# Attention with decay bias and a gated feed-forward block: projections in two runs of four per head, weighing in one run, maxima placed one head earlier

## What is computed

```python
qkv = layernorm(x) @ w_attn + b_attn            # 32 heads of width 16
scores = einsum('bqhd,bkhd->bhqk', q, k) / 16
scores = where(rel <= 0, scores + slopes * rel, -inf)   # rel = key position - query position
out = softmax(scores) @ v
x = x + out @ w_proj + b_proj
```

## Time and profile before

| | us |
|---|---|
| median of 3 runs | 922.75 |
| lowest, highest | 920.37, 922.88 |
| profiled execution | 921.12 |
| its span, first to last instruction | 919.4 |
| TensorE busy (matmul) | 860.3 |
| VectorE busy | 477.3 |
| ScalarE busy | 364.1 |
| GpSimd busy | 183.5 |

### The profile page before, as it was taken

The page is one execution under the profiler, slowest core; times in us unless marked ns, Lnnn a source line. Parts: engine busy times, 40 slices in busy tenths (PEclk is TensorE's granted clock), DMA queues, the critical chain, the costliest instruction groups (busy, mean ns, idle before and its releaser), DMA issues. The chain is left out here.

```text
span 919.4 us, 13759 instructions
## 1 busy us (share of the span) xinstructions
PE 860.3 (94%) x5088; PEld 580.1 (63%) x5088; DVE 477.3 (52%) x931; ACT 364.1 (40%) x693; POOL 183.5 (20%) x337
## 2 busy tenths in 40 slices
PE   1999799999999999999998579999999999999998
PEld 1755355556555565555543268887888788878886
DVE  6586577766777667776773154443222322232223
ACT  4345455565556655565555233322111211111111
POOL 4223233342433324333342300000000000000000
PEclk9999899999999999999999879999999999999999
DMA  8764445655565455735461364203000310021001
GB/s 267 207 208 140 122 146 170 185 155 161 177 207 164 137 171 186 227 112 170 143 207 49 113 227 155 89 0 137 2 1 1 96 41 0 0 77 60 0 0 46
DMA packets 70562, 109.33 MB, mean 119 GB/s; under 512 B 13395, under 2 KB 38662, under 8 KB 70505
## 3 DMA queue, kind: packets, MB, share of 16 engines
q1 hardware_dynamic: 68457, 108.32, 37.5%
q10 hardware_dynamic: 2048, 0.27, 0.2%
HBM read 65.97 MB, written 42.32 MB: 118 GB/s over the span
## 5 line engine op out<-in xcount | busy, mean ns | idle before, releaser
L839 DVE TENSOR_REDUCE bm<-bank 128x3 f32<-128x384 f32 (+1 forms) x384 | 223.0, 596 | 118.8 <-PE bank L1045 114.7
L700 ACT ACTIVATE pt<-bank 128x512 f32<-128x512 f32 (+1 forms) x384 | 196.8, 528 | 168.4 <-PE bank L1067 162.9
L1067 PE MATMUL bank<-q_st,k_st 116*128 116x512 bf16 (+3 forms) x512 | 136.7, 309 | 18.0 <-DMA q_st<-mt 10.5
L1336 DVE TENSOR_TENSOR gu<-bank,silu 128x512 f32<-128x512 f32 x44 | 30.5, 692 | 220.2 <-issue 132.7
L1147 PE MATMUL bank<-fT_hi,wgu_hi 128*128 128x512 f32 x352 | 138.8, 394 | 5.5 <-DVE wgu_lo L1308 3.5
L1043 PE MATMUL bank<-k_st,q_st 97*128 97x512 bf16 (+3 forms) x512 | 141.6, 302 | 0.8 <-DMA q_st<-slopes_dram 0.6
L1147 PE MATMUL bank<-fT_lo,wgu_hi 128*128 128x512 f32 x352 | 138.4, 393 | 0.0
L1147 PE MATMUL bank<-fT_hi,wgu_lo 128*128 128x512 f32 x352 | 137.7, 391 | 0.0
L1067 PEld LDWEIGHTS bank<-q_st,k_st 116*128 116x128 bf16 x512 | 41.7, 98 | 131.0 <-ACT pt L700 72.1
L1045 PE MATMUL bank<-mask_qk,identb 128*128 128x128 bf16 x512 | 106.4, 220 | 0.0
L610 POOL TENSOR_SCALAR_AFFINE_SELECT pt<-pt 128x256 f32<-128x256 f32 x128 | 52.7, 412 | 213.1 <-ACT pt L700 213.1
(11 more groups left out here) (95 smaller groups left out, 1217.0 us busy)
## 6 DMA issues: line engine op xcount, KB each, us to landing
stack_dram<-part SPq DMA_DIRECT2D x32, 384.0 KB, 2.6
q_st<-stack_dram SPq DMA_DIRECT2D x32, 384.0 KB
k_st<-stack_dram SPq DMA_DIRECT2D x32, 384.0 KB
stack_dram<-part SPq DMA_DIRECT2D x32, 256.0 KB, 3.1
pv_dram<-weighed SPq DMA_DIRECT2D x32, 256.0 KB, 4.8
weighed<-pv_dram SPq DMA_DIRECT2D x17, 256.0 KB
xt<-x SPq DMA_DIRECT2D x16, 256.0 KB, 4.3
stack_dram<-part SPq DMA_DIRECT2D x32, 128.0 KB, 3.9
```

The lines of the kernel that those rows point to most:

```text
L700: act.activation(pt[:, h % PT_RING, COL0[k]:COL0[k] + WIDE[k]], bank[3 + (3 * h + k) % 2][:, 0:WIDE[k]], ACT.Exp, scale=1.0 / HD).then_inc ...
L839: dve.tensor_reduce(bm[:, h % 4, BM_AT[k]:BM_AT[k] + BM_N[k]], bank[k][:, 0:BM_N[k] * P].rearrange("p (n q) -> p n q", q=P), AX.X, ALU.max ...
L1067: last = pe.matmul(bank[3 + u % 2][:, at:at + n], k_st[0:K_EXP, s, h % 4, t * P:(t + 1) * P], q_st[0:K_EXP, s, h % 4, t * P:S], start=True ...
L1336: dve.tensor_tensor(gu[:, f % 2, :], bank[5 + 2 * (f % 2)][:, :], silu[:, f % 2, :], ALU.mult).then_inc(gu_done, 1)
```

## The change

- TensorE, each head: the projections stand behind the shifted scores of k = 0 and k = 1, four each, ahead of the scores of the same k. Before they stood behind the scores, three, three and two.
- The pair of shifted scores of k = 1 is issued the other way round, 128 columns (t = 3) and then 384 (t = 1); each keeps its place in the bank.
- The weighing of the chunk before runs as a whole behind the scores of head 0, k = 1. Before, t = 0 stood there and the rest behind k = 2.
- The next chunk's maxima are transposed behind the scores of head 1, k = 0 (before: after head 1), copied behind the maximum of head 1, k = 1 (before: of head 2, k = 0), and placed after the exponentials of head 1 (before: of head 2).
- ScalarE copies the weighed values (`copy_pv`) after the third exponential of head 0; before, after the first of head 1.

```diff
@@ ScalarE
-                    if i == 1 and c > 0:
-                        copy_pv(c - 1)
...
                     exponential(h, 2)
+                    if i == 0 and c > 0:
+                        copy_pv(c - 1)
+                    if i == 1 and c + 1 < CHUNKS:
+                        place_maxima(c + 1)
...
                     if i == 2:
-                        if c + 1 < CHUNKS:
-                            place_maxima(c + 1)
@@ VectorE
                     scored(0)
-                    if i == 2 and c + 1 < CHUNKS:
-                        copy_maxima(c + 1)
                     if i == 3:
                         for tile in made(c)[:1]:
                             read_tile(*tile)
                     scored(1)
+                    if i == 1 and c + 1 < CHUNKS:
+                        copy_maxima(c + 1)
@@ shifted_scores
-                at = 0
-                for t in T_TILES[k]:
+                for t in T_TILES[k][::-1]:
                     n = S - t * P
+                    at = S - P if t == 3 else 0
...
-                    at += n
@@ TensorE
                         shifted_scores(h, k)
+                        if i > 0 and k < 2:
+                            between(c, 8 * (i - 1) + 4 * k, 8 * (i - 1) + 4 * k + 4)
                         scores(h + AHEAD, k)
-                        if i > 0:
-                            between(c, 8 * (i - 1) + 3 * k, 8 * (i - 1) + min(3 * k + 3, 8))
-                        if i == 0 and c > 0:
-                            if k == 1:
-                                weigh_values(c - 1, (0,))
-                            if k == 2:
-                                weigh_values(c - 1, (1, 3, 2))
+                        if (i, k) == (0, 1) and c > 0:
+                            weigh_values(c - 1, (0, 1, 3, 2))
+                        if (i, k) == (1, 0) and c + 1 < CHUNKS:
+                            transpose_maxima(c + 1)
...
-                    if i == 1 and c + 1 < CHUNKS:
-                        transpose_maxima(c + 1)
```

## The result

The changed kernel takes 915.32 us as the median of 20 runs, the kernel before 921.47 us beside it; the ratio is 0.9929, with a 95% interval of 0.9915 to 0.9942. That is 6.5 us less by the ratio and 6.2 by the medians. The prediction was 911 (899 to 921) and a gain of 10.7 by its sum: the sign and the range hold, the gain was forecast too large. The profiled execution took 915.61 us with a span of 913.9, 5.5 under that of before.

A forecast was written before the change was run, and what follows sets the result against it. TensorE, busy for 94% of the span, was taken as the bound. Terms -13.2 - 5.0 + 11.7 - 3.8 - 0.6 - 2.0 + 1.5 + 0.7 = -10.7 us gave 910.4 or 912.1, predicted as 911 us, range 899 to 921.

The forecast's parts named there:

- the projections: Two runs of four behind wide shifted scores save entry costs, 0.17 us per head in 26 x 3 heads: -13.2 us.
- the weighing: One run instead of two in first heads saves 0.2 us in each of 25 chunks (1, 4 to 27): -5.0 us.
- the held-up exponential: Later scores delay exponential (h,1): 1.03 us stalls ending nine chunks, 0.6 after 9, 17, 25; with chunk 1, +11.7 us.
- the stacks: K's later second part delays the stack loads for chunks 8, 16 and 24, 0.5 us taken each: +1.5 us.
- the cover of what stands behind it on VectorE: In chunk 2 of a batch, P's second tile enters earlier and the tokens' low part comes later: 0.25 us three times, +0.7.
- Chunk 1: At its end TensorE waits for VectorE's normalised tokens; the delayed remainder adds +0.6 us, with no clock priced.
- The chunks without projections: In chunks 2, 3 and 28 to 31 ScalarE bounds, so one weighing run gains 0 (-1 to +2).
- The maxima: Earlier placing removes waits in the loop's body: -3.8 us, with -0.6 at chunk 4 and -2.0 before chunk 30.
- 2 us more until the next chunk's first score: Issue on ScalarE's queue moves from 10.4 us into its chunk to about 7.8 of 13.7, leaving 2 us more for landing.
- Rival B: In the second head ScalarE's issue waits for VectorE's copy, TensorE pays in every chunk: 925 to 926 us, slower; chance 0.13.

The follow-up runs named there:

- the experiment that cuts it: The changed kernel with VectorE making a Q tile's remainder ahead of the block maximum of k = 0 in head 3: 907.31 us, ratio 0.9859.

## Why the prediction was right, and where it was off

The sign and the range held, and so did the mechanism of the three largest terms (the projections, the weighing, the held-up exponential); of the gain of 10.7 us 6.2 to 6.5 arrived. Between the two traces 5.2 us are missing: 3.6 in chunks 0 to 3, 2.3 in chunks 4 to 27 and 0.5 before the loop, less 1.1 that the end of the loop gave beyond its forecast. Two misses helped, and that is luck: the 1.5 us for the stacks were not due in this trace, and chunk 4's first head lost 1.1 us of lower clock.

**The projections: right, a little small.** Forecast 0.17 us a head, measured 0.17 in second heads (3.48 for 3.65) and 0.20 in third ones (3.20 for 3.40); the bounds from the mask and from the rows of chunk 31 carried over to tiles with scores in them, and the reversed order is worth what the prediction said it would be.

**The weighing: right in size, incomplete around it.** Forecast 0.2, measured 0.23 to 0.24 in most first heads (3.73). The step that failed is the cover of what stands behind it on VectorE: the prediction put 0.25 us on chunk 2 of a batch, three times. In the second and third heads of chunks 10, 18 and 26 the changed kernel has 4.16 and 3.68 us, where the sum gives 3.92 and 3.23: 0.7 together in each of these chunks. The low part of the tokens is late both times, once for the second transposes (0.24) and once for P's second tile (0.45). Chunk 10's third head, where P's second tile starts just after VectorE has written the low part (L815):

```profile
210.32 0.67 DVE L815 TENSOR_TENSOR fT_lo<-bank,fT_hi 128x512 fp32r<-128x512 f32 x1
...
211.09 0.47 PE L1003 MATMUL bank<-wproj_hi,aT_hi 128*128 128x512 f32 x1 [0.22 <-issue]
```

The sum had nothing for the chunks behind them, 12 and 20, either. Their first heads take 4.45 and 4.38 us (4.10 and 4.19 before) and their third ones 3.60 (3.40): in chunk 12 VectorE reads a P tile (L829) only after a wait of 1.51 us for GpSimd, the maximum comes behind it, and TensorE waits for that. Some 2 us together; no run here takes that apart.

```profile
231.23 0.69 DVE L829 TENSOR_TENSOR xr<-bank,xr 128x512 f32<-128x512 f32 x1 [1.51 <-POOL xr L619]
...
232.44 0.34 PE L1043 MATMUL bank<-k_st,q_st 97*128 97x384 bf16 x1 [0.54 <-DVE bm L839]
```

**The held-up exponential: right.** Forecast 4.25 for the last heads of nine chunks and of chunks 9, 17 and 25; measured 4.27 in eight of them, 4.36 in chunks 5, 13 and 21, and 5.00 in chunk 23, because VectorE there first waits 1.20 us for the load of the values that it divides. The chain was taken from the earlier trace rows alone, and the experiment that cuts it gives the time back.

**Chunk 1: right in kind, too small.** Forecast +0.6 for the tokens, measured +0.84 at the end of chunk 1. But the sum priced no clock for a longer wait, on the ground that 1.21 us had left it up. That was the argument for the new stalls of 1.0 us, and there it held: the clock stays up through all of them. The wait before chunk 2 was another one, 1.54 us in the kernel before and longer after, and I didn't look at it. It cost 1.7 us, the largest single miss.

**The chunks without projections: in the bounds.** Forecast 0 (-1 to +2). Placing in head 1 holds ScalarE by its 1.15 us where ScalarE is the bound: chunk 2's third head grows by 1.2 us and the last one falls by 0.8 (with the placement late again the third is back at 1.84). Its second head grows by 0.9 us too, but that belongs to the weighing: it takes 3.06 with the weighing alone and 3.04 with the placement late again. In chunks 28 and 29 the wait behind it had been longer, so there it gained 0.5 and 1.0.

**The maxima: half.** Forecast: all waits in the body of the loop go. Measured: from 10.5 to 5.9 us, 1.6 of it before the loop, 2.9 at chunk 4, 0.5 before chunk 30, and 0.25 and 0.63 left before chunks 12 and 20. At chunk 4 the wait is shorter only because TensorE comes later: the maxima land 56.6 us behind the loop's first score, 54.2 before. The step that failed is "2 us more until the next chunk's first score": it took the landing to move with the issue. Behind chunks with traffic in front it does not.

**The stacks: right, but hidden.** The 1.5 us are not in the changed kernel's trace; they appear as soon as the stalls in front are gone (0.98 in chunk 6), which is what the prediction's term was about.

**Rival B** did not come as a rule: third heads of chunks with projections are at 3.20 to 3.24, but for those with tokens (3.27 and 3.68), chunks 12 and 20 (above), and chunks 0 (3.68) and 16 (3.38). In these two it did come: the second of the two placing DMAs holds ScalarE's queue for 1.44 and 1.09 us there instead of its usual 0.61, the exponentials of head 2 come late, and TensorE waits for them. So the cover was enough by a narrow margin. Chunk 0 in the changed kernel:

```profile
61.91 1.98 ACTq L724 DMA_DIRECT2D q_st<-mt  x2
...
63.94 1.36 ACT L700 ACTIVATE pt<-bank 128x512 f32<-128x512 f32 x3 [2.24 <-PE bank L1067]
...
64.59 0.28 PE L1067 MATMUL bank<-q_st,k_st 116*128 116x256 bf16 x1 [0.23 <-ACT pt L700]
```

## What to carry to other kernels

When work is put in front of a producer, follow everything queued behind that producer's reader on the other engines: here four projections in front of the scores moved a maximum, and behind it a remainder, a rounding and an exponential, and by the forecast's sum 11.1 of the 18.2 us that the projections and the weighing were to bring went there again; moving the remainder brought 6.5 to 8 us back. A wide weight load should stand behind a matmul wide enough to cover it, and in a pair of unequal ones that is the second. An edit that shortens the loop shortens the time for every transfer in it, so the gain of one part may depend on another part that issues earlier.

## What the runs showed of the hardware

- Entering a run of fp32r products with 128x128 weights costs 0.06 to 0.07 us of TensorE's time behind a matmul of 128 columns (1.44 for 1.37 us over the same run), and nothing measurable behind 384 or 512 (1.14 us for a 512-wide score of 0.22 and four products of 0.23).
- Two 4 KB transfers issued 2.3 us earlier, with a DMA share of 0.71 until they had landed (0.41 in the kernel before), landed no earlier: 5.4 us for 2.8 to landing, the later one at 230.97 and 230.83.
- The two placing DMAs of 4 KB take 1.15 us of ScalarE's queue in most chunks, some 0.5 and 0.6 us each, and at times far more: 1.98 together in the changed kernel (61.91), 2.34 in the kernel before (152.59).
- Eight stalls of TensorE of 0.90 to 1.00 us at the ends of chunks, and one of 1.64 us before chunk 24, left the granted clock at its upper level; after a wait of 2.56 us it stood at 0.50 for 3.4 us, though TensorE was busy again by then.
